# Attention and RWKV-style mixing with layer norms on one core: inputs laid out by channel, VectorE's 32x32 transposes in place of TensorE's, ScalarE normalising the result, new places in the order

## The chip, the cores and the metric

One core of a Trainium2 chip runs the whole program. Time is device time in microseconds; the kernel before takes 707.49 us, the median of three runs (705.98 to 707.81). TensorE is also called PE, VectorE DVE, ScalarE ACT, GpSimd POOL and the SyncE queue SP, as in the profile.

## The reference, cut to what matters

Sixteen sequences x of 512 tokens by 128 channels, 16 heads of 8 channels, all in f32:

```python
h = x @ W1 + b1                      # 128 -> 384, per head q, k, v of 8 channels
w = softmax(causal(q @ k.T / sqrt(8)))
x = layernorm(x + (w @ v) @ Wp + bp)
x_prev = x shifted by one token
xr, xk = mu_r*x + (1-mu_r)*x_prev, mu_k*x + (1-mu_k)*x_prev
out = sigmoid(xr @ W_r.T) * (relu(xk @ W_k.T)**2 @ W_v.T)
x = layernorm(x + out)
```

## The kernel before, in words

Each sequence is a batch element and passes through seven stages, each one step behind the last: X (x is loaded and transposed), A (q and k, split into three bf16 parts that go out to memory and come back as operands), S (row maxima of the scores, and v), T (scores again, transposed, exponentials, product with v), D (division by the sums, projection, first layer norm, transpose), E (key, gate, value), F (second layer norm and store). `OFFSET` tells which batch element a stage has in step b. A step has ten groups g, five for each half of the heads; a group has two places.

The order of each engine is written out by hand, and every engine takes its instructions strictly in that order. TensorE does in each group, twice: a pair of T chunks (`t_chunks`, L559) into one of three banks `tps`, the masks and score matmuls of a pair of S chunks (L582, L597) into one of three banks `sps`, then whatever `SPARE_USES` puts at this place; and behind the second the product with v of the group before (`pv`, L624). A pair of S chunks waits by `bank_free` until all but the last chunk ahead of it is reduced.

VectorE does in each group: `reduce_chunk` 0 and 1 (L843), the small work of place 0, layer norm pieces, `reduce_chunk` 2 and 3, the work of place 1. ScalarE takes the exponentials of each T pair (L765), then copies of spare results. GpSimd does its pieces of the group and at its end the causal mask of the group's exponentials (`mask_group`, L1023), which `pv` needs.

All small matmul results share one PSUM bank, `spare`: each use waits until the one ahead of it is read. Seven of the fourteen uses per step are transposes by TensorE against an identity: xT (four of 128x128), max0 and max1 (row maxima of a half, 128x32), sums0 and sums1 (the unnormalised attention output of a half with its sums, four each), attnT (four), hT (four); the other uses are the matmuls q, k, v, project, key, gate and value.

The maxima of a half: TensorE transposes them, ScalarE negates them into `negmax` (L747), GpSimd splits them into two bf16 parts (`split_max`, L1036 and L1038), SP writes them to memory and loads them back as rows of `qop` (`load_max`, L388). The attention output of a half: ScalarE copies it (`copy_o`), TensorE transposes it, VectorE takes reciprocals and multiplies straight from PSUM (L873, L876); after both halves TensorE transposes once more and ScalarE copies attnT (L736). In group 4 VectorE adds bias and x into y (L882) and takes the moments; in group 5 GpSimd makes the inverse deviation (`inverse_deviation`, L1043 and L1045) and VectorE scales y to h in groups 5 and 6 (L894). The same helper scales z to the result in groups 3 and 5.

A step in the middle of the run repeats every 39.0 us. The first attention step has S only; after the last S step come one with T only and a finish written out by halves.

Of the kernel before, what the change touches and what calls it, by code (L numbers as in the profile page):

```python
# [26 lines left out]
BF16 = mybir.dt.bfloat16  # L27
# [4 lines left out]
P = 128  # L32
# [3 lines left out]
BLK = 128  # L36
HROWS = 64
# [12 lines left out]
MAXIMA = QUARTET * NQBLK  # L50
LOADED = 16 * 2 * 2
# [9 lines left out]
FIRST_STEP, LAST_STEP = -3, 17  # L61
# [9 lines left out]
}  # L71
LATE = ("T", "D", "E", "F")
EARLY_OPS = (("k", 0), ("xT", 1))
# [31 lines left out]
MOVED = {("sums1", BATCH - 1): (1, 1), ("attnT", BATCH - 1): (2, 1), ("key", BATCH - 2): (2, 0)}  # L105
# [28 lines left out]
def shifted(b, g, by):  # L134

    at = GROUPS * b + g + by
    return at // GROUPS, at % GROUPS, 0
# [42 lines left out]
def block_program(nc, x, W1, b1, Wp, bp, Wr, Wk, Wv, mu_r, mu_k, consts, out):  # L180
    with ExitStack() as ctx:
# [14 lines left out]
        w1 = sb("w1", [E, 3 * E])  # L196
        w1p = sb("w1p", [E, 3, E])
        wff = sb("wff", [E, 3, E])
        wffT = sb("wffT", [E, 3, E])
        wp = sb("wp", [E, E])  # L200
# [3 lines left out]
        bias = sb("bias", [P, 2 * E])  # L204
        vcol = sb("vcol", [E, 1])
        mus = sb("mus", [P, 2])
        half_power = sb("half_power", [P, TT])

        xa = sb("xa", [P, TT, E])
# [9 lines left out]
        negmax = sb("negmax", [MAXIMA, P])  # L219
        negmax_parts = sb("negmax_parts", [MAXIMA, MROWS, P], BF16)  # L220
# [3 lines left out]
        inv = sb("inv", [P, 2, TT, QUARTET, 2])  # L224
        attn = sb("attn", [P, TT, HEADS, DH])
# [7 lines left out]
        rstd = sb("rstd", [P, 2, TT])  # L233
        h = sb("h", [P, 2, TT, E])
# [39 lines left out]
        xa_in = sem("xa_in")  # L274
# [10 lines left out]
        s_reduced = sem("s_reduced")  # L285
        max_high = sem("max_high")
# [7 lines left out]
        o_copied = sem("o_copied")  # L294
        inv_done = sem("inv_done")
        xbias_done = sem("xbias_done")
# [13 lines left out]
        rstd2_done = sem("rstd2_done")  # L310
        result_done = sem("result_done")
# [63 lines left out]
        def _(sp):  # L375
            sp.dma_start(xa[:], x[0].rearrange("(t p) e -> p t e", p=P)).then_inc(xa_in, 16)
# [87 lines left out]
        def _(pe):  # L464
            def setup_rest():

                pe.wait_ge(weights_in, 16 * 7)
                for i in range(3):
                    last = nc.tensor.transpose(tps[:, 0, E * i:E * i + E], wff[:, i, :], ident)
# [675 lines left out]
```

## Time and profile before

| | |
|---|---|
| median of three runs | 707.49 us |
| profiled execution | 709.11 us |
| its span, first to last instruction | 707.4 us |
| mean granted TensorE clock | 0.935 of full |
| PE, DVE, ACT, POOL busy | 611.5, 546.1, 450.6, 415.5 us |
| DMA moved | 65.80 MB |

Busy time is the time in which an engine has an instruction under way; matmuls overlap, so a busy PE is not PE at its peak. The clock is 1.0 at 2.4 GHz and 0.5 at 1.2 GHz. In the timeline rows, the number in brackets is idle time of the engine before the instruction, with what ended it.

### The profile page before, as it was taken

The numbers are of one execution on the slowest core, as the hardware profiler recorded it, in microseconds if no ns is written. First come the engines' busy times: TensorE is split into PE (matmuls) and PEld (weight loads), VectorE is DVE, ScalarE is ACT, GpSimd is POOL, SyncE is SP. The second block draws the span as 40 slices with busy tenths as digits, with TensorE's granted clock in tenths as the row PEclk, the third lists the DMA queues.
The fourth block names the chain that finished last, engine by engine and source line by source line (L and its number), as shares of the span: only waits on it lengthen the run. The fifth ranks groups of instructions, "written<-read, shape, count | busy, mean of one in ns | idle before, by whom it ended". The sixth has DMA issues, their size and how long they took to land.

```text
span 707.4 us, 17691 instructions
## 1 busy us (share of the span) xinstructions
PE 611.5 (86%) x6729; PEld 273.8 (39%) x6729; DVE 546.1 (77%) x1654; ACT 450.6 (64%) x871; POOL 415.5 (59%) x548
## 2 busy tenths in 40 slices
PE   4458889989998999999899989989999999897963
PEld 2123333334343434444343434444443434342432
DVE  1386778789897988888897979888888979793237
ACT  2103777676767676767767677767677676666731
POOL 3011325565748485766757484857667575758473
PEclk9555999999999999999999999999999999997987
DMA  4752544333443535353334535353433335201100
GB/s 136 126 136 46 143 71 141 68 113 67 107 119 63 136 78 151 77 145 79 114 77 103 127 60 140 78 150 79 138 80 118 78 77 133 53 4 32 31 16 30
DMA packets 72202, 65.80 MB, mean 93 GB/s; under 512 B 9333, under 2 KB 63926, under 8 KB 72118
## 3 DMA queue, kind: packets, MB, share of 16 engines
q1 hardware_dynamic: 71410, 64.41, 38.3%
q8 instruction: 53, 0.87, 0.6%
q10 hardware_dynamic: 708, 0.26, 0.3%
q14 instruction: 31, 0.25, 0.1%
HBM read 34.70 MB, written 29.88 MB: 91 GB/s over the span
## 4 chain that ended last, share of the span: by engine, by line
PE 67%; DVE 20%; POOL 4%; ACT 4%; issue 3%; DMA 1%; ACTq 1%; POOLq 0%; SPq 0%; DVEq 0%
PE ops L624 18%; PE sps L597 13%; DVE rowmax L843 10%; PE tps L559 10%; PE spare L482 9%; PE spare L502 5%; PE sps L582 5%; DVE attn L876 2%; PE spare L534 2%; ACT probs L765 2%; DVE stats L849 2%; DVE y L882 1%; PE spare L497 1%; PE spare L523 1%; POOL probs L1023 1%
## 5 line engine op out<-in xcount | busy, mean ns | idle before, releaser
L843 DVE TENSOR_REDUCE rowmax<-sps 128x1 f32<-128x512 f32 (+7 forms) x1024 | 400.9, 450 | 85.7 <-PE sps L597 84.1
L765 ACT ACTIVATE probs<-tps 128x512 f32<-128x512 f32 x640 | 347.7, 597 | 122.6 <-PE tps L559 122.4
L1023 POOL TENSOR_SCALAR_AFFINE_SELECT probs<-probs 128x512 f32<-128x512 f32 x256 | 158.1, 636 | 205.6 <-ACT probs L765 204.2
L624 PE MATMUL ops<-probs,vop 128*32 128x384 f32 (+3 forms) x2048 | 175.6, 450 | 6.3 <-POOL probs L1023 5.8
L559 PE MATMUL tps<-qop,kop 50*128 50x384 bf16 (+3 forms) x1024 | 127.3, 307 | 13.7 <-ACT probs L765 11.2
L597 PE MATMUL sps<-kop,qop 48*64 48x512 bf16 (+7 forms) x2048 | 130.4, 310 | 8.1 <-DMA kop<-d_parts 8.1
L582 PE MATMUL sps<-qmask,dup 64*128 64x128 bf16 (+1 forms) x640 | 70.0, 215 | 27.1 <-DVE rowmax L843 24.5
L624 PEld LDWEIGHTS ops<-probs,vop 128*32 128x32 f32 x2048 | 50.7, 110 | 91.6 <-issue 62.2
L559 PEld LDWEIGHTS tps<-qop,kop 50*128 50x128 bf16 x1024 | 34.3, 94 | 125.6 <-ACT probs L765 82.9
L1030 POOL TENSOR_TENSOR qk_parts<-qk_rest,qk_parts 128x512 bf16<-128x512 f32 x32 | 36.8, 1152 | 46.8 <-ACT qk_parts L775 46.8
L597 PEld LDWEIGHTS sps<-kop,qop 48*64 48x64 bf16 x2048 | 43.1, 106 | 47.5 <-issue 18.5
L582 PEld LDWEIGHTS sps<-qmask,dup 64*128 64x128 bf16 x640 | 31.4, 95 | 75.9 <-DVE rowmax L843 71.7
L1055 POOL TENSOR_SCALAR scaled<-step_d,mus 128x512 f32<-128x512 f32 x30 | 47.2, 1573 | 1.5
L502 PE MATMUL spare<-xT,w1p 128*128 128x512 f32 x62 | 39.6, 724 | 2.7 <-ACT xT L727 2.7
L865 DVE SCALAR_TENSOR_TENSOR qk_rest<-spare,bias,qk_parts 128x512 f32<-128x512 f32 x31 | 23.3, 751 | 21.4 <-ACT qk_parts L743 21.4
L1057 POOL TENSOR_TENSOR mixed<-scaled,hT 128x512 f32<-128x512 f32 x30 | 38.0, 1266 | 2.5
L743 ACT ACTIVATE qk_parts<-spare,bias 128x512 bf16<-128x512 f32 x31 | 21.3, 688 | 27.5 <-PE spare L502 27.5
L1045 POOL TENSOR_TENSOR rstd<-vareps,half_power 128x4 f32<-128x4 f32 x30 | 31.5, 1050 | 2.5
L534 PE MATMUL spare<-mixed,wffT 128*128 128x512 f32 x28 | 16.7, 680 | 13.6 <-DVE attn L876 13.6
L873 DVE RECIPROCAL inv<-spare 128x32 f32<-128x32 f32 x32 | 11.2, 349 | 21.5 <-PE spare L518 21.5
L518 PE MATMUL spare<-cst,osum 128*128 128x128 f32 x128 | 21.9, 296 | 1.6 <-ACT osum L771 0.8
L482 PE MATMUL spare<-w1p,xT 128*128 128x128 f32 x128 | 19.4, 297 | 3.6 <-DVE attn L876 3.6
(123 smaller groups left out, 571.7 us busy)
## 6 DMA issues: line engine op xcount, KB each, us to landing
qop<-d_parts SPq DMA_DIRECT2D x64, 192.0 KB, 4.5
kop<-d_parts SPq DMA_DIRECT2D x63, 192.0 KB, 5.3
d_parts<-qk_parts SPq DMA_DIRECT2D x15, 768.0 KB, 3.4
d_parts<-qk_parts SPq DMA_DIRECT2D x15, 512.0 KB, 4.4
d_parts<-qk_parts SPq DMA_DIRECT2D x17, 256.0 KB, 4.6
xa<-L_attn_x SPq DMA_DIRECT2D x16, 256.0 KB, 2.8
xres<-L_attn_x SPq DMA_DIRECT2D x16, 256.0 KB, 3.1
out<-result SPq DMA_DIRECT2D x15, 256.0 KB, 2.4
```

Source lines behind the costliest of these rows:

```text
L482: last = nc.tensor.matmul(spare[:, P * t:P * t + P], tokensT[:, P * t:P * t + P], weights, start=True, stop=True)
L502: last = nc.tensor.matmul(spare[:], w1p[:, "qk".index(use), :], xT[:, n % BANKS], start=True, stop=True)
L559: last = nc.tensor.matmul(tps[:, bank(n + k), off:off + w], kop[r, par, pair, BLK * a:BLK * a + BLK], qop[r, par, pair, BLK * a:SEQ], star ...
L582: nc.tensor.matmul(dst, dup[r, :], src, start=True, stop=False, skip_group_check=True)
L597: last = nc.tensor.matmul(sps[out:out + QBLK, bank(n + k), off:off + w], qop[r, par, pair, QBLK * a:QBLK * a + QBLK], kop[r, par, pair, 0: ...
L624: last = nc.tensor.matmul(ops[32 * t:32 * t + 32, BLK * a:SEQ], vop[:, par, a, QUARTET * half + t, hh, :], probs[:, g % 2, i, off:off + w] ...
L765: nc.scalar.activation(probs[:, g % 2, i, :], tps[:, bank(n), :], ACT.Exp, scale=SCALE)\
L843: last = nc.vector.reduce_max(rowmax[:, par, QUARTET * half + i, a:a + 1], sps[:, bank(n), off:off + w], axis=AX_X)
L1023: last = nc.gpsimd.affine_select(out=v, in_=v, compare_op=ALU.is_ge, fill=0.0, base=0, pattern=[[0, QUARTET], [1, BLK]], channel_multiplie ...
L1030: nc.gpsimd.tensor_tensor(part(i, 2), qk_rest[:, i, :], part(i, 1), ALU.subtract).then_inc(qk_split, 1)
L1055: nc.gpsimd.tensor_scalar(scaled[:], step_d[:], mus[:, i:i + 1], None, ALU.mult).then_inc(scaled_done, 1)
L1057: nc.gpsimd.tensor_tensor(mixed[:, i, :], scaled[:], hT[:, 0:SEQ], ALU.add).then_inc(mixed_done, 1)
```

## The change

- Host: x comes a second time transposed per sequence, and is loaded straight into xT; W1 comes sorted into q, k, v; the feed-forward weights come transposed; biases and mu come as one table of columns. The stage X has no TensorE or ScalarE work left, and the first step, -3, is gone.
- Maxima: VectorE turns the 128x32 maxima in 32x32 squares (`turn_maxima`), in group 5 and in group 0 of the next step, behind the group's first two reductions. They are no longer negated; the constant rows that meet them are -1. GpSimd splits them at the start of groups 5 and 0. Four DMAs take the place of one on the way out.
- Attention output: VectorE turns 128x512 in squares (`turn_sums`, groups 2 and 7), takes reciprocals, divides (`divide`, groups 3 and 8) and turns back straight into attnT (`turn_back`, group 3).
- The second layer norm's scaling goes to ScalarE (groups 4 and 5), as scale and shift; GpSimd makes the shift.
- Places: v, hT, gate, value, ksq, z, the mixing and the splits of q and k move by a group or a place.

```diff
-FIRST_STEP, LAST_STEP = -3, 17
+FIRST_STEP, LAST_STEP = -2, 17
 SPARE_USES = {
-    ("X", "xT"): (6, 1),
     ("A", "q"): (0, 1), ("A", "k"): (1, 1),
-    ("S", "v"): (9, 0), ("S", "max0"): (6, 0),
-    ("T", "max1"): (1, 0), ("T", "sums0"): (8, 1),
-    ("D", "sums1"): (2, 0), ("D", "attnT"): (3, 0), ("D", "project"): (4, 0), ("D", "hT"): (8, 0),
-    ("E", "key"): (2, 1), ("E", "gate"): (5, 0), ("E", "value"): (7, 0),
+    ("S", "v"): (8, 1),
+    ("D", "project"): (4, 0), ("D", "hT"): (7, 0),
+    ("E", "key"): (2, 1), ("E", "gate"): (3, 1), ("E", "value"): (5, 1),
 }
...
@@ sync @@
-            sp.dma_start(xa[:], x[0].rearrange("(t p) e -> p t e", p=P)).then_inc(xa_in, 16)
+            sp.dma_start(xT[:, 0], xT_in[0]).then_inc(xT_loaded[0], 16)
...
-                sp.dma_start(d_max[half].rearrange("i h r q -> r i h q"),
-                             negmax_parts[:].rearrange("r i (h q) -> r i h q", h=2)).then_inc(max_out, 16)
+                for hh in range(2):
+                    for part in range(2):
+                        r = HROWS * hh + SQUARE * part
+                        sp.dma_start(d_max[half, :, hh, :, SQUARE * part:SQUARE * part + SQUARE].rearrange("i r q -> r i q"),
+                                     max_parts[r:r + SQUARE]).then_inc(max_out, 16)
...
@@ scalar @@
+            def normalise(n, half):
+                wait(act, shift2_done, n + 1)
+                wait(act, stored, 16 * n)
+                for t in tiles_of(half):
+                    last = nc.scalar.activation(result[:, t, :], z[:, t, :], ACT.Identity, bias=shift[:, t:t + 1],
+                                                scale=rstd[:, 1, t:t + 1])
...
@@ vector @@
+            def turn_maxima(n, half):
+                wait(dve, s_reduced, 4 * GROUPS * n + 2 * GROUPS * (half + 1))
+                wait(dve, max_split, 2 * n + half)
+                nc.vector.transpose(maxT[:], rowmax[:, n % 2, QUARTET * half:QUARTET * half + QUARTET, :].rearrange(
+                    "p a b -> p (a b)")).then_inc(max_turned, 1)
+            def turn_sums(n, half):
+                m = 2 * n + half
+                wait(dve, o_copied, m + 1)
+                wait(dve, attn_done, m)
+                nc.vector.transpose(turned[:].rearrange("q b s h d -> q (b s h d)"), osum[:, half, :])\
+                    .then_inc(turned_done, 1)
+                wait(dve, turned_done, m + 1)
+                nc.vector.reciprocal(inv[:, half], turned[:, :, 1, :, 0]).then_inc(inv_done, 1)
+            def divide(n, half):
+                m = 2 * n + half
+                wait(dve, inv_done, m + 1)
+                wait(dve, attnT_done, n)
+                nc.vector.tensor_tensor(attn[:, :, half], turned[:, :, 0],
+                                        inv[:, half].unsqueeze(3).to_broadcast([P, SQUARES, 2, DH]), ALU.mult)\
+                    .then_inc(attn_done, 1)
+            def turn_back(n):
+                wait(dve, attn_done, 2 * n + 2)
+                is_written(dve, "project", n - 1)
+                nc.vector.transpose(attnT[:], attn[:].rearrange("q b s h d -> q (b s h d)")).then_inc(attnT_done, 1)
...
@@ vector, step(b), behind reduce_chunk 0 and 1 @@
+                    if g == CHUNKS and active("S", b):
+                        turn_maxima(before("S", b), 0)
+                    if g == 0 and active("S", b - 1):
+                        turn_maxima(before("S", b - 1), 1)
                     for _, use, n in ORDER[b, g, 0]:
                         spare_use(use, n)
+                    if tg == 2 and active("D", tb):
+                        turn_sums(before("D", tb), 1)
+                    if tg == 3 and active("D", tb):
+                        divide(before("D", tb), 1)
+                        turn_back(before("D", tb))
+                    if tg == CHUNKS + 2 and active("T", tb):
+                        turn_sums(before("T", tb), 0)
+                    if tg == CHUNKS + 3 and active("T", tb):
+                        divide(before("T", tb), 0)
...
-                    if tg in (3, 5) and active("F", tb) and before("F", tb) < LAST - 1:
-                        n = before("F", tb)
-                        wait(dve, stored, 16 * n)
-                        normalise(1, n, (tg - 3) // 2, z, result, rstd2_done, result_done)
...
@@ gpsimd, step(b) @@
+                    if g == CHUNKS and active("S", b):
+                        split_max(before("S", b), 0)
+                    if g == 0 and active("S", b - 1):
+                        split_max(before("S", b - 1), 1)
                     if tg == 0 and active("E", tb) and before("E", tb) < LAST:
-                        mix_sum(before("E", tb), 0)
+                        mix_add(before("E", tb), 0)
                     if tg == 1 and active("F", tb) and before("F", tb) < LAST - 1:
                         inverse_deviation(1, before("F", tb), moments2_done, vareps2_done, rstd2_done)
+                        shift_of(before("F", tb))
-                    if g in (2, 3) and active("A", b):
-                        split_low(before("A", b), g - 2)
+                    if g in (3, 4) and active("A", b):
+                        split_low(before("A", b), g - 3)
...
-                    if tg == 4 and active("E", tb) and before("E", tb) < LAST:
+                    if tg == 3 and active("E", tb) and before("E", tb) < LAST:
                         n = before("E", tb)
                         is_read(pool, "key", n)
...
                     if tg == 5 and active("D", tb) and before("D", tb) < LAST:
                         inverse_deviation(0, before("D", tb), moments_done, vareps_done, rstd_done)
-                    if tg == 8 and active("E", tb) and before("E", tb) < LAST - 1:
+                    if tg == 6 and active("E", tb) and before("E", tb) < LAST - 1:
...
+                    if tg == 8 and active("D", tb) and before("D", tb) < LAST:
+                        mix_step(before("D", tb))
+                        mix_scale(before("D", tb), 1)
                     if tg == 9 and active("D", tb) and before("D", tb) < LAST:
-                        mix_step(before("D", tb))
-                        mix_sum(before("D", tb), 1)
+                        mix_add(before("D", tb), 1)
+                        mix_scale(before("D", tb), 0)
```

## Rows read from the trace of the kernel before

**Rows 1.** The page, part 1: busy us and share of the span.
```profile
PE 611.5 (86%) x6729; PEld 273.8 (39%) x6729; DVE 546.1 (77%) x1654; ACT 450.6 (64%) x871; POOL 415.5 (59%) x548
```

**Rows 2.** The page, part 4: the chain that ended last, by engine.
```profile
PE 67%; DVE 20%; POOL 4%; ACT 4%; issue 3%; DMA 1%; ACTq 1%; POOLq 0%; SPq 0%; DVEq 0%
```

**Rows 3.** Windows of one steady step: length, busy us of PE, PEld, DVE, ACT, POOL, clock, DMA.
```profile
294.00:333.00 39.00, 36.28 (x424) 16.49 (x420) 33.47 (x102) 27.89 (x55) 26.12 (x35) 1.00 0.43 105
```

**Rows 4.** Timeline of PE, groups 2 and 5 to 7 of a steady step: start, us, instruction.
```profile
302.37 0.66 PE L518 MATMUL spare<-cst,osum 128*128 128x128 f32 x4
302.96 0.39 PE L559 MATMUL tps<-qop,kop 50*128 50x512 bf16 x2
...
304.86 1.12 PE L534 MATMUL spare<-mixed,wffT 128*128 128x512 f32 x2 [1.00 <-DVE attn L876]
...
313.45 0.39 PE L559 MATMUL tps<-qop,kop 50*128 50x512 bf16 x2
314.41 0.20 PE L582 MATMUL sps<-qmask,dup 64*128 64x64 bf16 x2 [0.57 <-DVE rowmax L843]
...
318.50 0.28 PE L478 MATMUL spare<-cst,rowmax 128*32 128x128 f32 x1
...
321.51 0.39 PE L559 MATMUL tps<-qop,kop 50*128 50x512 bf16 x2
```

**Rows 5.** Timeline of DVE in the same step.
```profile
303.81 0.35 DVE L873 RECIPROCAL inv<-spare 128x32 f32<-128x32 f32 x1
...
304.73 1.41 DVE L843 TENSOR_REDUCE rowmax<-sps 128x1 f32<-128x384 f32 x4
...
312.03 0.69 DVE L882 TENSOR_TENSOR y<-spare,xbias 128x512 f32<-128x512 f32 x1 [0.37 <-PE spare L482]
...
314.99 1.29 DVE L843 TENSOR_REDUCE rowmax<-sps 128x1 f32<-128x512 f32 x2 [0.30 <-PE sps L597]
316.23 0.60 DVE L894 TENSOR_SCALAR h<-y,moments,rstd 128x128 f32<-128x128 f32 x2
```

**Rows 6.** Groups by form: busy us, mean ns, of a 128x256 tensor operation.
```profile
L967 DVE TENSOR_TENSOR step_d<-hT 128x256 f32<-128x256 f32 x2 | 0.8, 414 | 0.0
```

**Rows 7.** Timeline of POOL in the same step.
```profile
314.75 0.24 POOL L1043 TENSOR_SCALAR vareps<-moments 128x4 f32<-128x4 f32 x1
315.07 1.05 POOL L1045 TENSOR_TENSOR rstd<-vareps,half_power 128x4 f32<-128x4 f32 x1
...
322.19 0.29 POOL L1036 TENSOR_SCALAR negmax_parts<-negmax 32x128 bf16<-32x128 f32 x1
322.56 0.42 POOL L1038 TENSOR_TENSOR negmax_parts<-negmax,negmax_parts 32x128 bf16<-32x128 f32 x1
```

**Rows 8.** Windows of other stretches, columns as in rows 3.
```profile
117.00:120.00 3.00, 1.97 (x28) 0.75 (x24) 2.66 (x11) 2.15 (x5) 2.50 (x4) 1.00 0.35 124
...
121.00:127.00 6.00, 6.00 (x45) 1.91 (x41) 4.28 (x12) 3.29 (x7) 1.93 (x4) 0.50 0.77 127
...
642.00:645.00 3.00, 1.22 (x16) 0.48 (x16) 0.00 (x0) 2.26 (x5) 2.93 (x4) 1.00 0.00 0
...
646.00:656.00 10.00, 8.15 (x31) 2.19 (x34) 1.49 (x7) 5.43 (x11) 6.95 (x11) 0.50 0.02 4
```

**Rows 9.** Timeline of PE in step 1, around the clock's fall.
```profile
117.10 0.39 PE L559 MATMUL tps<-qop,kop 50*128 50x512 bf16 x2
...
127.16 0.39 PE L559 MATMUL tps<-qop,kop 50*128 50x512 bf16 x2
```

**Rows 10.** Timeline of all engines at the start.
```profile
4.31 1.09 PE L497 MATMUL spare<-cst,xa 128*128 128x128 f32 x4 [4.31 <-DMA cst<-shape_constants]
...
8.12 2.07 PE L502 MATMUL spare<-xT,w1p 128*128 128x512 f32 x2 [2.73 <-ACT xT L727]
```

**Rows 11.** Timelines of ACT and PE in the tail.
```profile
682.00 0.59 ACT L771 COPY osum<-ops 128x512 f32<-128x512 f32 x1 [5.24 <-PE ops L624]
...
687.05 0.71 PE L652 MATMUL spare<-wp,attnT 128*128 128x128 f32 x4 [0.68 <-ACT attnT L736]
```

More of the change, by code:

```diff
@@ L491, in spare_use @@
                     pe.wait_ge(s_reduced, 4 * GROUPS * BATCH)
-                if use == "xT":
-                    wait(pe, xa_in, 16 * (n + 1))
+                if use in ("q", "k"):
+                    wait(pe, xT_loaded[n % BANKS], 16 * (n // BANKS + 1))
+                    if n == 0:
+                        pe.wait_ge(w1_in, 16)
+                    last = nc.tensor.matmul(spare[:], w1p[:, "qk".index(use), :], xT[:, n % BANKS], start=True, stop=True)
+                elif use == "v":
+                    last = tokens_by_weights(spare, xT[:, n % BANKS], w1p[:, 2, :])
+                elif use == "project":
+                    wait(pe, attnT_done, n + 1)
+                    last = tokens_by_weights(spare, attnT, wp[:])
+                elif use == "hT":
@@ L654, in by_weights @@
                 return last
-            is_read(pe, "attnT", LAST)
+            wait(pe, attnT_done, LAST + 1)
             for half in range(2):
@@ L722, in spare_use @@
                 spare = spares[k]
-                if use in ("max0", "max1"):
-                    wait(act, max_split, 2 * n + int(use[-1]))
                 is_written(act, use, n)
-                if use == "xT":
-                    ins = nc.scalar.copy(xT[:, n % BANKS], spare[:])
-                elif use == "v":
+                if use == "v":
                     if n == 0:
@@ L734, in spare_use @@
                                          spare[:].rearrange("k (a h d) -> k a h d", h=2, d=DH))
-                elif use == "attnT":
-                    ins = nc.scalar.copy(attnT[:], spare[:])
                 elif use in ("q", "k"):
@@ L742, in spare_use @@
                     wait(act, parts_out, 48 * (n - 1))
[L743 removed]
+                    nc.scalar.activation(part(i, 0), spare[:], ACT.Identity, bias=scalars[:, i:i + 1])\
                         .then_inc(qk_high, 1)
                     return
[L746 to L747 removed]
                 elif use == "hT":
@@ L864, in spare_use @@
                     wait(dve, qk_split, 2 * (n - 1) + i + 1)
-                    last = nc.vector.scalar_tensor_tensor(qk_rest[:, i, :], spare[:], bias[:, i:i + 1], part(i, 0),
+                    last = nc.vector.scalar_tensor_tensor(qk_rest[:, i, :], spare[:], scalars[:, i:i + 1], part(i, 0),
                                                           ALU.add, ALU.subtract)
-                elif use in ("sums0", "sums1"):
-                    half = int(use[-1])
-                    is_written(dve, use, n)
-                    is_written(dve, "attnT", n - 1, k)
-                    tiles = spare[:].rearrange("q (t r s h d) -> q s t r h d", t=TT, r=QUARTET, s=2, h=2)
-                    nc.vector.reciprocal(inv[:, half], tiles[:, 1, :, :, :, 0]).then_inc(inv_done, 1)
-                    wait(dve, inv_done, 2 * n + half + 1)
-                    for t in range(TT):
-                        last = nc.vector.tensor_tensor(
-                            attn[:, t, DH * half:DH * half + DH].rearrange("q (r h) d -> q r h d", h=2),
-                            tiles[:, 0, t], inv[:, half, t].unsqueeze(3).to_broadcast([P, QUARTET, 2, DH]), ALU.mult)
                 elif use == "project":
```

203 lines of the change are left out of this document (90 added, 113 removed).

## The prediction

> **What bounds the kernel now.** I read the page's busy shares first, then the chain of waits, then one steady step by windows, and last the timeline of that step engine by engine. TensorE is the busiest (86% of the span), VectorE second with 77% [rows 1], and the chain runs 67% through PE and 20% through DVE [rows 2]. A steady step lasts 39.0 us: the window of that length holds 36.28 us of PE, 33.47 of DVE, 27.89 of ACT, 26.13 of POOL, at full clock [rows 3]. So PE idles 2.7 us a step, and its longest gap is 1.00 us ahead of the key matmul, where it waits for VectorE's attn product [rows 4].
>
> The shares alone mislead. Scores live in three banks and go in pairs of chunks, 20 pairs a step. PE may start the mask matmul of a pair once VectorE has reduced the *first* chunk of the pair before (the idle of 0.57 us at 314.41 is this wait [rows 4]), and VectorE starts about 0.6 us after that mask matmul (314.41 to 314.99 [rows 4, 5]). A pair takes VectorE 1.41 us, or 1.29 [rows 5]. The two engines thus stay within one chunk of each other, and a pause of either longer than that is passed to the other. I carried this rule through the 20 pairs, with each engine's order and the durations of the rows: it gives 38.9 us for the step of before, where the rows say 39.0, so I use it for the changed order.
>
> **The change, part by part** (per steady step, unless said)
> 1. *PE.* Gone are the x, two sums and the attn transposes, four sets of four at 0.59 us (302.37 to the next instruction at 302.96), and two of the maxima at 0.28 [rows 4]: 4 x 0.59 + 2 x 0.28 = 2.9 us. The 1.00 us wait of key goes too, since no spare bank is held by the attn product. If PE set the step alone: 39.0 - 3.9 = 35.1.
> 2. *VectorE.* Gone: two times reciprocal and products (303.81 to 304.73, 0.92 us each) and the result's four scalings (as h's, 0.60 per two, 0.51 without overlap; [rows 5]) : 1.84 + 1.02 = 2.9 us. Added: three 32x32 transposes of 128x512. The trace has none. Below: 0.35, as the short reciprocal; above: 1.38, two passes at the 0.69 of the 128x512 sum; I take 0.65, the latter less overlap [rows 5]. Two divisions of 128x256 at 0.41 [rows 6], two reciprocals at 0.35, two 128x32 transposes at 0.18 (between nothing and 0.35), and five waits for its own results at 0.04: 1.95 + 0.82 + 0.70 + 0.36 + 0.20 = 4.0. Net +1.1: VectorE now carries about 34.6 to 35.0 and PE 33.4. The bound moves to VectorE.
> 3. *Coupling.* VectorE's new work falls behind the first pair of groups 2, 3, 7 and 8, each time ahead of the next reduction, and PE has nothing queued that it may do instead, because the S pair is next on its queue. Carried through the 20 pairs, and before part 4 is put in, PE now waits 0.4 to 0.6 us at most pairs and the step is 38.9 us: the 2.9 us off PE return as short waits. Gain 0.1.
> 4. *A new wait in group 5, the one that decides.* Before, POOL in group 5 makes 1/deviation right behind its mask: 314.75 plus 0.32, then 1.05 us, done at 316.12 [rows 7]; VectorE wants it for h at 316.23 [rows 5]: hidden by a hair. After, VectorE turns the maxima in group 5 *behind* its first two reductions; POOL's split of these maxima stands in group 5 *ahead* of 1/deviation; and VectorE's h stands directly behind its own turning. So h waits for a chain that starts only when VectorE reaches it: split 0.37 + about 0.33 (the second instruction is on 32 columns now, 0.42 before), then 0.32 + 1.05, and 0.14 of handovers = 2.2 us of VectorE standing still [rows 7]. What is queued behind it: h, reductions 2 and 3 of the group, gated; who waits: PE's masks of group 6. By hand, from the step's start: mask of group 5 at 21.2, turned at 23.2, h from 25.5 to 26.0, first reduction done 26.6; PE, ready for group 6's mask at 25.3, starts it at 26.7 and waits 1.2 us again at its second pair. Next step begins at 40.9. Bounds of the wait: 1.7 (both split instructions as short as vareps, 0.24) to 2.4 (the old durations); the step 40.4 to 41.1. Both conditions hold in steps 1 to 14: 14 times, +1.9 us each.
> 5. *TensorE's clock.* With the stall, PE in the stretch from 24.5 to 28.4 of the step works about 40% of the time, by the same table. Rows of before: behind 642:645 with 1.22 us of work in 3 the granted clock is 0.50, that is 1.2 GHz, and it fell once in the middle of the run too, behind 117:120 with 1.97 in 3; it then stood at half for 6 us of full work [rows 8]. What one fall costs is a difference of rows: group 5 to 7, from 117.10 to 127.16, took 10.06 us [rows 9], the same stretch of a steady step 313.45 to 321.51, 8.06 [rows 4]: +2.0 us. I take one fall in each of the 14 steps (from none to one): 42.9 us a step. Ends: 0 and +3.5 (all of PE's 6.4 us at half, nothing hidden).
>    The Trainium skill says the same of such kernels (TensorE: Matmul & The Clock Gate, A second HAM failure mode: psum-queue depth-cycling): cycling through PSUM banks leaves TensorE idle between groups often enough that the clock swings. By that rule every step falls, and the sum is as here; a reader who trusts the steady step more than the rule, whose gap of 1.00 us left the clock full, gets rival A.
> 6. *Other moves.* ScalarE loses the copies of xT and attnT and two of the maxima, and gains four scalings of 128x128: within 1 us of its 27.9, hidden since it has 11 us of idle [rows 3]; without that cover 0.3. POOL gains two tiny instructions and has mixing spread over groups 8, 9 and 0; mask(9) then ends about 1 us before PE wants it. Bound 0 to +0.5. SP: the maxima go out in four DMAs for one per half, some 1 us more issue and at most 1 us of landing; they are split two groups earlier and wanted half a step later; 0. The x load no longer waits for a transpose; 0. key, gate, value, hT, v earlier: PE does the same work in other groups, 0 to -0.2. Parts of q and k leave one group later, 3.5 us, with over 10 us to spare: 0.
> 7. *Start.* x transposes, ScalarE's table load and its copy stand between 4.31 and q at 8.12 [rows 10]. q can then start when x and W1 are in, an estimated 1.1 us after 4.31, so 2.7 earlier; but the table load stays in the chain, now in front of q's first activation. -2.0 (-2.7 to 0). The prologue step without attention: the turned maxima add 0.2, the x transposes leave 0.1: 0. Step 0 has no h and so no wait; it loses 1.7 us of PE transposes and adds about as much to VectorE as it drops: -0.5 (-1.7 to +0.5).
> 8. *Tail.* From the last osum copy (682.00) to the projection (687.05) are 5.05 us [rows 11]; copy 0.59, turn 0.69, reciprocal 0.35, divide 0.42, turn back 0.69 and hops 0.25 make 3.0: -2.0. Step 15 loses transposes where POOL and ACT partly cover them: -1.5 (0 to -4).
>
> Sum, against the profiled execution's 709.1: 14 x (1.9 + 2.0) = 54.6; -0.5 - 2.0 - 3.5 = -6.0; together 757.7. The profiled execution lies 1.6 above the median of the runs, so the forecast for the median is 756.
>
> **Rivals**
> - *A: the wait is there, the clock holds.* For: steady steps keep the full clock with a 1.00 us gap [rows 3, 4]. Against: the new stretch has less work than either stretch ahead of a fall, in proportion, or as little [rows 8]. 709.1 + 26.6 - 6.0 - 1.6 = 728.
> - *B, faster: the pause is absorbed.* If the pairs couple less than my table has it (a reduction freed earlier, PE further ahead), the step is VectorE's sum plus the wait, 35.0 + 2.2 = 37.2, 1.8 under 39.0: 709.1 - 25 - 6.0 - 1.6 = 676. The point from which it decides: VectorE's other idle, 3.6 us a step in my table, must fall under 1.7. Against it: the table reproduces 39.0, and VectorE idles 5.5 us a step before [rows 3]. If only the wait of part 4 were missing, the step stays 38.9 and the run comes to about 700.
> - *C: transposes of f32 take two passes.* 3 x 0.65 more on VectorE; by hand 0.9 a step beyond the wait, as part fills idle: 756 + 13 = 769. For it: no row has this operation. Against: every 128x512 operation of VectorE in the trace takes one pass, 0.69.
>
> **How the numbers follow.** Forecast 0.55, A 0.22, B 0.15 (676 to 704), C 0.08. A measurement tells about 0.3% from no change; with that bound faster 0.16, same 0.03, slower 0.81. The range leaves out B and what of C and the full cost of the falls lies above: 712 to 772; the forecast's own is 742 to 770.
>
> **What would show it.** In the changed profile: DVE's h idle before it, released by POOL's rstd, about 2.2 us, 14 times; steps of 42 to 43 us; PEclk under 1.0 once a step; PE's share under 80% and DVE's share about 80%; 128x512 transposes near 0.7 us; no PE transposes but h's; key without its 1.00 us. I am wrong in the main step if h waits under 1 us or steps are under 39; wrong in the clock if PEclk stays at 1.0 from 80 to the tail; wrong in the rate if a transpose takes over 1 us.

## The result, and the profile after

The changed kernel takes 738.78 us (736.61 to 743.37, 4 runs) beside 707.65 (705.98 to 708.61) for the kernel before: ratio 1.0464, 95% interval 1.0427 to 1.050. Slower, inside the forecast's range and 17 us under its 756. The wait of part 4 is there at the size forecast. Part 5, the clock, is not the other half of the loss: it comes to some 6 us in place of 28, and a collision of VectorE with GpSimd, which the prediction did not have, stands beside it. Every ratio rests on executions that lie within 1.5% of the fastest of their kernel.

The page of the changed kernel: busy us, granted clock in 40 slices, the chain by engine [rows 1, 2].
```profile
PE 599.7 (81%) x6438; PEld 254.2 (34%) x6438; DVE 567.8 (77%) x1579; ACT 455.0 (61%) x862; POOL 415.6 (56%) x576
PEclk9999997697999999999999999999999999999975
PE 55%; DVE 27%; issue 7%; POOL 5%; ACT 4%; DMA 1%; DVEq 0%; POOLq 0%; SPq 0%; ACTq 0%
```
PE gave up 11.8 us of busy time, VectorE took on 21.7, and the chain moved from PE (67 to 55%) to VectorE (20 to 27%). VectorE's share stayed at 77%, because the span grew with the work.

What was waited for in the changed kernel: engine and line, releaser, us in total, times, longest.
```profile
PE sps L557 <- DVE rowmax L809: 68.2, 105, 2.5
DVE h L877 <- POOL rstd L1043: 33.0, 15, 2.5
```
The second row is part 4; the first is how it reaches PE. Timeline of VectorE in group 5 and 6 of a late step [rows 5].
```profile
416.53 0.20 DVE L848 STREAM_TRANSPOSE maxT<-rowmax 128x32 f32<-128x32 f32 x1
418.92 0.84 DVE L877 TENSOR_SCALAR h<-y,moments,rstd 128x128 f32<-128x128 f32 x2 [2.19 <-POOL rstd L1043]
```
The same on GpSimd [rows 7]: it waits for the turned maxima, splits them, and only then makes 1/deviation.
```profile
416.82 0.22 POOL L1028 TENSOR_SCALAR max_parts<-maxT 128x32 bf16<-128x32 f32 x1 [1.70 <-DVE maxT L848]
417.12 0.25 POOL L1030 TENSOR_TENSOR max_parts<-maxT,max_parts 128x32 bf16<-128x32 f32 x1
417.45 0.23 POOL L1041 TENSOR_SCALAR vareps<-moments 128x4 f32<-128x4 f32 x1
417.77 1.05 POOL L1043 TENSOR_TENSOR rstd<-vareps,half_power 128x4 f32<-128x4 f32 x1
418.79 0.64 POOL L1015 TENSOR_SCALAR_AFFINE_SELECT probs<-probs 128x512 f32<-128x512 f32 x1
```
TensorE pays in group 6 [rows 4]:
```profile
420.42 0.23 PE L557 MATMUL sps<-qmask,dup 64*128 64x128 bf16 x2 [1.39 <-DVE rowmax L809]
...
422.28 0.29 PE L557 MATMUL sps<-qmask,dup 64*128 64x128 bf16 x2 [0.96 <-DVE rowmax L809]
```

**Where the 34.2 us of span are** (741.6 against 707.4). The q matmul opens each step. The windows from q to q, after [rows 3]:
```profile
97.01:143.54 46.53, 39.22 (x388) 14.62 (x384) 32.97 (x90) 26.32 (x50) 21.08 (x29) 0.78 0.38 87
143.54:187.51 43.97, 38.10 (x406) 15.61 (x402) 35.17 (x99) 27.05 (x51) 24.42 (x32) 0.88 0.33 82
187.51:229.63 42.12, 35.60 (x406) 14.99 (x402) 35.10 (x99) 28.42 (x56) 26.11 (x36) 0.96 0.42 96
229.63:271.19 41.56, 34.32 (x407) 14.94 (x403) 35.11 (x99) 28.50 (x56) 26.12 (x36) 1.00 0.41 98
271.19:311.97 40.78, 35.74 (x406) 15.45 (x402) 34.33 (x99) 28.36 (x56) 26.16 (x36) 0.96 0.40 100
352.76:395.83 43.07, 35.87 (x407) 15.34 (x403) 35.09 (x99) 28.54 (x56) 26.10 (x36) 0.96 0.40 94
```
Twelve steps, from 97.01 to 602.15, take 505.1 us where before's twelve, from 100.77 to 568.38, took 467.6: +37.5. All ahead of them is 3.8 shorter, all behind them 0.4 longer. Now read clock against length. The step at full clock takes **41.56**, and one with a fall can take *less*, 40.78. What differs is VectorE's busy time: 35.11 against 34.33, 0.78 us, the very difference of the two lengths. It is one instruction pair, the h of group 6. VectorE in these two steps, the h of groups 5 and 6:
```profile
252.72 0.84 DVE L877 TENSOR_SCALAR h<-y,moments,rstd 128x128 f32<-128x128 f32 x2 [2.19 <-POOL rstd L1043]
...
256.61 1.36 DVE L877 TENSOR_SCALAR h<-y,moments,rstd 128x128 f32<-128x128 f32 x2
...
294.28 0.84 DVE L877 TENSOR_SCALAR h<-y,moments,rstd 128x128 f32<-128x128 f32 x2 [2.19 <-POOL rstd L1043]
...
298.16 0.59 DVE L877 TENSOR_SCALAR h<-y,moments,rstd 128x128 f32<-128x128 f32 x2
```
Counted from q, the first pair stands at 23.09 in both steps and the second at 26.98 and 26.97: the fall, from 21.3 to 24.7 us into the second step, has held VectorE up by nothing, and the lengths part at the second pair alone. GpSimd in the same stretches:
```profile
255.44 1.27 POOL L1092 TENSOR_TENSOR z<-gated,h 128x512 f32<-128x512 f32 x1 [2.21 <-DVE gated L842]
256.65 1.23 POOL L1015 TENSOR_SCALAR_AFFINE_SELECT probs<-probs 128x512 f32<-128x512 f32 x2
...
296.99 1.27 POOL L1092 TENSOR_TENSOR z<-gated,h 128x512 f32<-128x512 f32 x1 [2.21 <-DVE gated L842]
298.62 1.23 POOL L1015 TENSOR_SCALAR_AFFINE_SELECT probs<-probs 128x512 f32<-128x512 f32 x2 [0.37 <-ACT probs L726]
```
Each row of h and of masks is two instructions. In the long case the first h begins within 0.05 us of the first of two masks of GpSimd, and each h ends 0.08 us behind its mask, the second at 257.97 against 257.89. In the short case PE at half clock was late with the scores in group 6, so ScalarE's exponential came late, GpSimd stood idle for 0.37 us, and h got in between and took 0.59. At 418.92 one of two h waits likewise for the end of a mask (419.43): 0.84. The mean h was 354 ns before, 516 after. VectorE's reductions and its 128x512 transposes (0.70 us) took no longer beside a mask than without one.

The Trainium skill states a mechanism (SBUF — State Buffer, "SBUF: two separate sides"): VectorE in some modes and GpSimd take a shared port pair as an exclusive lock for a whole instruction, whichever of them starts first, and the other blocks fully. The rows agree with it in the end, 0.08 us behind the mask. They do not show the part on who starts first: in the long case the record of the first h begins 0.05 us ahead of the mask's, and h is the one held. No run here isolates the port.

### The profile page after: what moved, and what is told of

Read it like the earlier page. It is cut to its first block, busy times and chain, and to the rows that moved or that the text cites. A ratio compares the mean times of both kernels' runs of the same rounds, so it can differ in the third digit from the quotient of the medians.

```text
span 741.6 us, 17178 instructions
## 1 busy us (share of the span) xinstructions
PE 599.7 (81%) x6438; PEld 254.2 (34%) x6438; DVE 567.8 (77%) x1579; ACT 455.0 (61%) x862; POOL 415.6 (56%) x576
## 4 chain that ended last, share of the span: by engine, by line
PE 55%; DVE 27%; issue 7%; POOL 5%; ACT 4%; DMA 1%; DVEq 0%; POOLq 0%; SPq 0%; ACTq 0%
DVE rowmax L809 16%; PE ops L599 16%; PE sps L572 12%; PE spare L481 7%; PE tps L534 7%; PE sps L557 5%; PE spare L495 5%; ACT probs L726 2%; POOL rstd L1043 2%; PE spare L509 2%; DVE stats L815 2%; DVE h L877 2%; DVE y L836 1%; DVE turned L856 1%; DVE moments L819 1%
## 5 line engine op out<-in xcount | busy, mean ns | idle before, releaser
L599 PE MATMUL ops<-probs,vop 128*32 128x384 f32 (+3 forms) x2048 | 186.5, 474 | 5.3 <-POOL probs L1015 4.1
L534 PE MATMUL tps<-qop,kop 50*128 50x384 bf16 (+3 forms) x1024 | 131.0, 315 | 34.9 <-ACT probs L726 34.1
L877 DVE TENSOR_SCALAR h<-y,moments,rstd 128x128 f32<-128x128 f32 x60 | 28.6, 516 | 33.0 <-POOL rstd L1043 33.0
L1053 POOL TENSOR_SCALAR scaled<-step_d,scalars 128x512 f32<-128x512 f32 x30 | 47.1, 1571 | 3.1
L1028 POOL TENSOR_SCALAR max_parts<-maxT 128x32 bf16<-128x32 f32 x32 | 7.0, 219 | 67.1 <-DVE maxT L848 67.0
L495 PE MATMUL spare<-xT,w1p 128*128 128x512 f32 x62 | 39.6, 724 | 4.5 <-DMA w1p<-W 4.5
L831 DVE SCALAR_TENSOR_TENSOR qk_rest<-spare,scalars,qk_parts 128x512 f32<-128x512 f32 x31 | 23.3, 751 | 19.7 <-ACT qk_parts L706 19.7
L706 ACT ACTIVATE qk_parts<-spare,scalars 128x512 bf16<-128x512 f32 x31 | 21.3, 687 | 27.7 <-PE spare L495 27.7
L856 DVE STREAM_TRANSPOSE turned<-osum 128x512 f32<-128x512 f32 x32 | 22.4, 700 | 16.0 <-ACT osum L732 16.0
L1092 POOL TENSOR_TENSOR z<-gated,h 128x512 f32<-128x512 f32 x14 | 17.8, 1269 | 29.5 <-DVE gated L842 29.5
L698 ACT COPY vop<-spare 128x512 f32<-128x512 f32 x16 | 9.4, 587 | 39.4 <-PE spare L481 39.4
```

The lines of the kernel that those rows point to most:

```text
L495: last = nc.tensor.matmul(spare[:], w1p[:, "qk".index(use), :], xT[:, n % BANKS], start=True, stop=True)
L534: last = nc.tensor.matmul(tps[:, bank(n + k), off:off + w], kop[r, par, pair, BLK * a:BLK * a + BLK], qop[r, par, pair, BLK * a:SEQ], star ...
L599: last = nc.tensor.matmul(ops[32 * t:32 * t + 32, BLK * a:SEQ], vop[:, par, a, QUARTET * half + t, hh, :], probs[:, g % 2, i, off:off + w] ...
L877: last = nc.vector.tensor_scalar(dst[:, t, :], src[:, t, :], moments[:, i, t, 0:1], rstd[:, i, t:t + 1], ALU.subtract, ALU.mult)
L1053: nc.gpsimd.tensor_scalar(scaled[:], step_d[:], mus[:, i:i + 1], None, ALU.mult).then_inc(scaled_done, 1)
```

## The experiments

Each stands against the kernel before, timed beside it on the same chip: 706.28 us for 1, 2, 4 and 6; 706.3 for 3, 5, 7 and 8; 706.04 for 9 and 12; 705.06 for 10 and 11. Ratios of different groups are compared only roughly. Steps are from q to q; kernel 1 is that of experiment 1, and so on.

**1. 1/deviation first.** The changed kernel with GpSimd's `inverse_deviation` of group 5 moved ahead of the split.
```diff
-                    if g == CHUNKS and active("S", b):
-                        split_max(before("S", b), 0)
                     ...
                     if tg == 5 and active("D", tb) and before("D", tb) < LAST:
                         inverse_deviation(0, ...)
+                    if g == CHUNKS and active("S", b):
+                        split_max(before("S", b), 0)
```


> The changed kernel with one edit: in group 5 GpSimd makes the inverse deviation ahead of the split of the maxima instead of behind it. Theory (the wait of h behind the split, 2.2 us in each of 14 steps, and the clock's falls that it brings): h waits under 0.1 us, a step falls from 42.1 us on average (40.8 where the clock holds) to 38.8 by the hand-carried table, the clock stays at 1.0 in the middle of the run; total 695 to 704 us, that is below the kernel before. Rival (VectorE is overloaded by its own transposes and the new places, and the wait only stands where it would idle anyway): at most a few us are won, total 730 or more.

704.68 us, ratio 0.9978 (0.9952 to 1.0004). Two windows of it:
```profile
211.93:250.73 38.80, 34.15 (x406) 14.93 (x402) 34.15 (x99) 28.37 (x56) 26.21 (x36) 1.00 0.44 106
250.73:291.05 40.32, 35.67 (x407) 15.46 (x403) 34.15 (x99) 28.38 (x56) 26.21 (x36) 0.96 0.42 100
```
One swap of two calls gives back the whole loss: h is at 362 ns and waits only once (2.5 us), so the swap takes away the wait and the collision together and does not tell them apart. It also shows parts 1 to 3: without the wait the 2.1 us less of PE's work bring 0.2 (39.00 to 38.80; by hand 38.9). The clock did not stay up as expected, it fell in two steps of the middle, and the total is 0.7 us over the range. So the run prices a fall of the clock that nothing hides: 1.5 us.

**2. Before, with the wait alone.** GpSimd's 1/deviation waits for the second reduction of group 5, close to where the turning of the maxima releases it after the change.
```diff
+                        wait(pool, s_reduced, 4 * GROUPS * before("S", b) + 4 * CHUNKS + 2)
                         inverse_deviation(0, before("D", tb), moments_done, vareps_done, rstd_done)
```


> The kernel before with only the wait put in: in group 5 GpSimd's inverse deviation first waits until VectorE has reduced the group's second chunk, so that VectorE's h finds it about 1.5 us late. Nothing else is changed. Theory: the table gives 40.4 us for a step of 39.0, so +20 us from the wait alone, 728, and up to 745 with falls of the clock. Rival (the transposes and places cost, not the wait; TensorE's queue covers a pause of VectorE): 707 to 712.

759.58 us, ratio 1.0744 (1.0697 to 1.0791): over the 728 to 745 expected. The wait itself is 24.0 us in 15, so 1.6 each.
```profile
266.80:310.19 43.39, 39.12 (x425) 17.30 (x421) 33.90 (x103) 28.14 (x55) 26.17 (x35) 0.92 0.38 93
310.19:352.50 42.31, 37.72 (x425) 16.88 (x421) 33.77 (x103) 28.13 (x55) 26.18 (x35) 0.96 0.40 96
```
The wait alone, with nothing else of the change, makes the kernel slower than the change does. Table 40.4, measured 42.3 with the clock at half for 3.4 us of the step, and 43.4 with 6.8 us. The first h also meets a mask (0.25 us more). PE still has its transposes here (37.7 to 39.1 us of work a step), which makes it likely that the falls are not hidden, but no full step of this run kept the clock, so how much of the +3.3 is wait and how much clock is argued from the table.

**3. A longer chain.** Three more small GpSimd instructions ahead of the split in group 5.
```diff
+                if half == 0:
+                    for k in range(3):
+                        nc.gpsimd.tensor_scalar(again[:, k], maxT[:], 1.0, 0.0, ALU.mult, ALU.add)
```


> The changed kernel with three more GpSimd instructions of the split's size in group 5, ahead of the split: the chain in front of h is longer by 3 x 0.3 = 0.9 us. Theory (every us of that chain stands in the step): h waits 3.1 us in place of 2.2, the table gives 41.6 for 40.7, 13 us more in all, and some more from the clock: 750 to 760. Rival (the wait is partly idle time that VectorE has anyway): under 5 us more than the changed kernel's 739.

763.98 us, ratio 1.0833 (1.0789 to 1.0878). They took 0.57 us together, not 0.9, and VectorE's wait grew from 2.19 to 2.71. Steps went to 42.7 and 42.9, later 44.5, with the clock at 0.96, 0.92 and 0.88: of +1.1 to +3.0 us a step over 41.56, 0.5 is the wait; the rest came with the falls (no step here kept the clock). The wait follows the chain; the total lies 4 us over the range.

**4. PE's work put back.** Kernel 1 with sixteen 128x128 transposes a step that nobody reads.
```diff
+                if use in ("v", "project", "hT", "value"):
+                    for t in range(TT):
+                        nc.tensor.transpose(spare[:, P * t:P * t + P], ident, ident)
```


> As e1, and TensorE gets 16 more 128x128 transposes a step (4 ahead of each of v, project, hT and value, into the shared bank, overwritten at once), 2.36 us, about the work that the change took from it. Theory (TensorE and VectorE are coupled pair by pair, VectorE is the fuller): the table gives 40.6 against 38.8 for e1, so about +25 us, since these four places are ones where VectorE's next pair is waited for. Rival (VectorE alone is the bound and TensorE idles 6 us a step): within 5 us of e1.

721.21 us, ratio 1.0206 (1.015 to 1.0261). 16.5 us over kernel 1, for about 25 expected. Steps at full clock 39.98, so +1.2 (table +1.8); with a fall 41.58, so 1.6 for one.
```profile
178.45:218.43 39.98, 35.73 (x422) 16.48 (x418) 34.09 (x99) 28.51 (x56) 26.16 (x36) 1.00 0.42 101
```
The sixteen transposes fill 1.58 us of PE (35.73 against 34.15), 0.40 per four, where part 1 counted 0.59 from start to start.

**5. Turns made twice.** Kernel 1 with the 128x512 transpose of each half done twice.
```diff
+                nc.vector.transpose(turned_again[:], osum[:, half, :])
                 nc.vector.transpose(turned[:].rearrange("q b s h d -> q (b s h d)"), osum[:, half, :])\
```


> As e1 (704.7), and VectorE's turn of the 128x512 attention output is done twice for each half, 2 x 0.63 us of VectorE a step more. Theory (pairwise coupling, VectorE the fuller engine but with waits of its own): the table gives 39.6 for 38.8, about +12 us, two thirds of the work added (20 us). Rival 1 (VectorE's sum is the bound): all of it, +20. Rival 2 (VectorE has slack, TensorE is the bound): under 5.

728.54 us, ratio 1.0316 (1.0273 to 1.036). 1.4 us more of VectorE a step makes the step at full clock 39.47, +0.67 (table 39.6); then the clock falls in nearly every step (41.00), in some twice (42.45). The total was missed, +24 us for +12, because the falls came in number, and here nothing covers them: 1.5 us each.

**6. `pv` inside the group.** Kernel 1 with `pv` at the first place of groups 2, 3 and 8 and q at (0, 0): TensorE then has work between the two pairs where VectorE has extra.
```diff
+                        if i == 0 and g in (2, 3, 8) and active("T", tb):
+                            pv(before("T", tb), tg - 1)
```


> As e1, with the same work in two other places of TensorE's queue: in groups 2, 3 and 8 the product with v stands between the group's two score pairs instead of behind both, where it followed a spare matmul directly; q moves to place 0 of group 0. Theory (the step is set by how far the two engines can run apart, not by either's sum): the table gives 37.0 for a step against 38.8, so 25 us less than e1: about 673. Rival (VectorE's sum is the bound, or GpSimd's masks come too late for the earlier products): no gain over e1, or a loss.

683.85 us, ratio 0.9661 (0.9608 to 0.9714): steps 36.90 at full clock (table 37.0), 38.44 with a fall. The step is as the table has it; the total is 11 us over the expected 673, with a fall in four of twelve steps. Part 3's coupling is what ate the gain: 1.9 us a step return when the order fits.

**7. Group 6 filled.** The changed kernel with ten idle matmuls of 128x512 in PE's waits of group 6.
```diff
+                        if g == CHUNKS + 1 and active("S", b) and active("D", b):
+                            fill(before("T", b), g, i)
```


> The changed kernel, and TensorE does 10 idle matmuls of 128x512 in group 6 of steps 1 to 14 while it waits for VectorE (6 ahead of the first score pair, 4 ahead of the second, into a score bank that the next chunk overwrites). The order and the wait of h stay. Theory (of the 39 us between the changed kernel and e1's order 28 are the wait and 10 to 14 the clock that falls in it): h still waits 2.2 us, the clock stays at 1.0 in the middle, steps of 40.8 to 41.0, total 724 to 730. Rival (the clock's falls are hidden behind VectorE, their price is nothing): 738 or more.

744.26 us, ratio 1.0538 (1.0475 to 1.0601). A miss on both counts. The clock still fell in every second step, half of the times from 21.3 us on, in group 5, behind two waits of 0.57 and 0.46 us and ahead of the filled ones. Steps with a fall took 42.0 and 42.15, and even those at full clock took 41.55, not 40.8.

**8. VectorE's small work spread.** Kernel 1 with the pieces placed singly between the 40 reductions of a step (only the two pairs of h stay together), places of the spare uses and `pv` shifted to match.
```diff
+VECTOR_AT = {'tm1': 1, 'qrest': 2, 'krest': 5, 'ts1': 7, 'rc1': 8, 'div1': 11, 'back': 14, 'y': 17, 'mom1': 19, 'gated': 21, 'tm0': 22, 'h0': 27, 'h1': 27, 'ts0': 32, 'rc0': 34, 'div0': 36, 'mom2': 39}
...
+                for slot in range(4 * GROUPS):
+                    reduce_chunk(before("S", b), slot // 4, slot % 4)
+                    for name, at in VECTOR_AT.items():
+                        if at == slot and work[name][0]:
+                            work[name][1]()
```


> As e1, with the same instructions in other places, chosen by the table: VectorE's small pieces stand singly between single reductions instead of together behind the second or fourth; q, k, key and value move to place 0 and hT to place 1 of their groups; the product with v stands inside groups 3, 7 and 8. Theory (the loss lies in how the two engines wait for each other pair by pair, not in their sums): 34.9 a step for 38.8, 14 x 3.9 = 55 less than e1: 650, at most 660, and the clock holds as TensorE is 93% busy. Rival (e6's gain of 21 was all that there is, ScalarE or GpSimd bound next): 675 to 685.

653.08 us, ratio 0.9249 (0.9204 to 0.9294), the best here.
```profile
203.03:238.61 35.58, 33.06 (x403) 14.72 (x403) 34.39 (x98) 27.96 (x55) 26.34 (x37) 1.00 0.45 114
```
VectorE works 34.39 of 35.58 us: now it is the bound, and the step is 3.4 us under before's 39.0. The edit moves TensorE's pieces too, and no run parts the two. Of VectorE's time 1.1 us a step is not work: one of the two divisions begins beside GpSimd's mixing and takes 1.49 us, where 0.41 is its time alone in the changed kernel.
```profile
232.03 1.49 DVE L877 TENSOR_TENSOR attn<-turned,inv 128x256 f32<-128x256 f32 x1
...
231.96 1.27 POOL L1073 TENSOR_TENSOR mixed<-scaled,hT 128x512 f32<-128x512 f32 x1
```
So the best order here still holds a collision of the kind that lengthened h.

**9. Groups 4 to 6 filled**, against experiment 7's open question.
```diff
-                        if g == CHUNKS + 1 and active("S", b) and active("D", b):
+                        if g in (CHUNKS - 1, CHUNKS, CHUNKS + 1) and active("S", b) and active("D", b):
```


> The changed kernel with idle matmuls of 128x512 (results overwritten, never read) ahead of TensorE's score masks: two at both places of group 4, three at both of group 5, six and four in group 6. This closes the two waits of about 0.5 us in group 5, behind which the clock fell even with group 6 filled, as well as those of 1.39 and 0.96 us in group 6. VectorE's order and its 2.2 us wait are untouched. If the falls cost what the same trace says (steps of 40.8 us where the clock stays up, 41.8 on average), the clock now stays at 1.0, every step is 40.8 to 41.0 and the run is 722 to 732. If the clock has no part in the length (steps above 40.8 have another cause), the run stays at 737 to 746 with the clock at 1.0. If filling brings no clock either, 740 to 750.

746.92 us, ratio 1.0575 (1.0537 to 1.0613).
```profile
223.45:265.76 42.31, 38.35 (x427) 16.66 (x423) 35.11 (x99) 28.60 (x56) 26.06 (x36) 1.00 0.39 96
```
The clock stays up in ten of twelve steps, and they take 42.31 each: no gain. The filler of group 4 stands where no wait was, so this run alone left its own cost open.

**10. Group 5 alone filled; 11. groups 5 and 6.** Two fillers at each place of group 5; in the second also five and three in group 6. The edit of kernel 11, against kernel 9:
```diff
-                for _ in range({4: 2, 5: 3, 6: 6 - i}[g]):
+                for _ in range(2 if g == CHUNKS else 5 - i):
```


> The changed kernel with two idle matmuls of 128x512 (overwritten, never read) ahead of TensorE's score masks at both places of group 5 only, where it waits 0.57 and 0.46 us for VectorE. They fit into these waits, so they cost nothing by themselves; the waits of 1.39 and 0.96 us in group 6 stay open. In the changed kernel the steps took 40.8 us where the clock stayed up and 42.1 on average over steps 3 to 14. If the clock falls because of the waits in group 5, and its fall is what lengthens these steps, the steps are 40.8, the clock is 1.0 and the run is 720 to 728. If the falls come from group 6 as well, 730 to 745 with the clock under 1.0.

> As the kernel with group 5 filled, and five and three idle matmuls ahead of the masks in group 6 too, so that nearly no wait is open in the stretch. Steps of 40.8 to 41.2 and 720 to 732 if the clock's falls are the rest of the slowdown and the filler hides in the waits; 738 or more at a clock of 1.0 if it was not the clock that made the steps longer than 40.8 but something else, or if even hidden filler costs. In the run with group 4 filled too, steps were 42.3 at a clock of 1.0, which leaves both open.

Kernel 10 spread widely: 740.29, 743.96, 752.05 and 763.48 us; its ratio, from the first two, is 1.0517 (1.0439 to 1.0594). Kernel 11 takes 740.11 us, ratio 1.0496 (1.0434 to 1.0558). Kernel 11:
```profile
180.09:221.65 41.56, 36.89 (x419) 15.93 (x415) 35.12 (x99) 28.50 (x56) 26.12 (x36) 1.00 0.39 97
304.78:346.92 42.14, 38.18 (x418) 16.05 (x415) 35.12 (x99) 28.50 (x56) 26.12 (x36) 0.96 0.41 97
```
Six of eleven steps keep the full clock and all six take 41.56 or 41.57, to the hundredth what the changed kernel's own full-clock step takes; 738 or more at a clock near 1.0 is the branch "not the clock". The profile of kernel 10 is of its run of 752.05 us, at a clock of 0.906 on average, but its five full-clock steps are 41.56 too. In neither does the clock fall at 21.3 us any more, where five of the changed kernel's falls were; behind the first step, those that are left come from 26.3 us on. In both VectorE is busy 35.12 us a step: h collides every time, as nothing delays GpSimd's mask. The expected 40.8 rested on reading the changed kernel's 40.8 steps as undisturbed ones; they are the ones in which a fall hides in VectorE's stall *and* breaks the collision.

**12. Spread, with the change's order on GpSimd.** Kernel 8 with the split ahead of 1/deviation again (the edit of experiment 1 reversed); VectorE now has five reductions between turning and h.

> The spread order (its run before: 653.08 us) with GpSimd's order of the change put back: the split of the maxima stands ahead of 1/deviation in group 5 again. VectorE now turns the maxima in slot 22 of 40 and scales h in slot 27, five reductions (over 3 us) later, and the chain split plus 1/deviation takes 2.2 us. If what costs is the distance on VectorE between what releases the chain and what waits for it, h waits under 0.5 us and the run is within 0.4% of 653. If the order on GpSimd itself costs (it delays mask and key's square behind the split), the run is 660 to 685.

667.01 us, ratio 0.9419 (0.9358 to 0.948), 14 over kernel 8. h no longer waits (0.8 us in all), yet the distance theory fails and the rival's range holds it: the step is 36.27, and 37.17 with a fall, which comes in five of twelve. GpSimd, in order, now stands at the split itself, and all behind it is late:
```profile
222.59 0.22 POOL L1044 TENSOR_SCALAR max_parts<-maxT 128x32 bf16<-128x32 f32 x1 [1.92 <-DVE maxT L857]
...
226.41 1.22 POOL L1031 TENSOR_SCALAR_AFFINE_SELECT probs<-probs 128x512 f32<-128x512 f32 x2
```
so that on VectorE the four h again meet the late z and mask, and take 1.85 us (1.42 in kernel 8):
```profile
226.11 1.85 DVE L889 TENSOR_SCALAR h<-y,moments,rstd 128x128 f32<-128x128 f32 x4
```

## Why the prediction was right, and where not

The direction and the main cause were right: by the forecast's own sum the wait alone gives 728, which is inside the range. That the time came within 17 us of 756 is partly luck, since 28 us for the clock were too much and the collision was missing.

- *Part 1, PE.* PE fell from 36.28 us a step to 34.32 at full clock: 2.0, not 2.9, since four transposes fill 0.40 and not 0.59 (experiment 4). The error cost nothing, as part 3 gave the gain away. Key's 1.00 us wait is gone.
- *Part 2, VectorE.* Taken 0.65, 0.18 and 0.41 for the transposes and the division; measured, by form:
```profile
L742 ACT ACTIVATE result<-z,shift,rstd 128x128 f32<-128x128 f32 x56 | 24.3, 490 | 0.0
L856 DVE STREAM_TRANSPOSE turned<-osum 128x512 f32<-128x512 f32 x32 | 22.4, 700 | 16.0 <-ACT osum L732 16.0
L865 DVE TENSOR_TENSOR attn<-turned,inv 128x256 f32<-128x256 f32 x32 | 15.5, 483 | 0.1
L848 DVE STREAM_TRANSPOSE maxT<-rowmax 128x32 f32<-128x32 f32 x32 | 6.5, 202 | 0.0
```
  One pass, so rival C falls. The division's 483 ns are a mean, mostly of 414 alone and 564 beside GpSimd's square of key. VectorE grew by 0.7 us a step without the collision (34.15 in kernel 1) and 1.6 with it; forecast 1.1.
- *Part 3, coupling.* Right: 38.80 without the wait (forecast 38.9). Experiments 6 and 8 show it from the other side.
- *Part 4, the wait.* Right: 2.19 us, 14 steps, and 40.78 (forecast 40.9) in the steps whose fall and missing collision leave the wait alone; the first pair of h, 0.84 us for 0.59, is in it. The lower bound was added wrongly: both split instructions at 0.24 give 2.0, not 1.7. Rival B falls.
- *Part 5, the clock: the step that failed.* Forecast one fall a step at +2.0, 28 us. Falls came in eight of the ten steps from 187.51 to 602.15, each 3.4 us long, but mostly not from the stretch that part 5 blamed. Five began 21.2 to 21.6 us behind q, in group 5, before PE's waits of 1.39 and 0.96 us in group 6; two began at about 26.4, as the second of these waits ended; one at 35.3. Two steps had the same waits and kept the clock. The price was a row of before whose fall lasted 6.8 us (120.3 to 127.1). An uncovered fall of 3.4 us costs 1.5 to 1.6 (experiments 1, 4, 5), also from 21.4 us on. In the changed kernel it depends on the place: from 21.2 to 21.4 us, in VectorE's stall of 2.2 us, it costs nothing and takes the collision away (40.78; at 21.6 us half of it, 41.12); from 26.4 it costs 0.5 (42.12, 42.09); from 35.3, 1.5 (43.07). The ten steps take 414.6 us, one *less* than ten at 41.56. The long falls of the first two steps (46.53 and 43.97; 20.5 and 10.2 us at half clock) cost 7.4 against two at 41.56; the same two steps of kernel 11, with one short fall each, take 41.20 and 42.10. So the clock made about 6 us net.
- *What stood in its place:* the collision, +0.78 in a step, which no part had. Per full-clock step: 38.80, +1.98 for the wait, +0.78 for h = 41.56. The split of the last two is read off the traces, no run takes the collision alone away; that every full-clock step of kernels 7, 10 and 11 is 41.56 too, at 35.1 us of VectorE, goes with it. Rival A (728: wait there, clock holding) is nearer to the mechanism than the forecast, and 11 us short. That 14 x 0.78 is 11 too is partly chance: the full collision stands in seven of the 14 steps, and falls of the clock lengthen others.
- *Part 6.* ScalarE's scalings took 490 ns each, 24.3 us in all, and were hidden as forecast (ACT 28.36 to 28.50 a step, from 27.89); no run tests them alone.
- *Part 7, start.* q starts at 4.52 instead of 8.12 [rows 10], the next q at 23.93 instead of 26.90: -3.0 (forecast -2.0). The 1.1 us that the forecast let pass from 4.31 to q were 0.2.
- *Part 8, tail.* Copy to projection:
```profile
716.72 0.59 ACT L732 COPY osum<-ops 128x512 f32<-128x512 f32 x1 [6.10 <-PE ops L599]
...
720.09 1.22 PE L627 MATMUL spare<-wp,attnT 128*128 128x128 f32 x4 [1.49 <-DVE attnT L872]
```
  3.37 us for 5.05 [rows 11]: -1.7 (forecast -2.0).

What stays open: which resource holds h and the division (the rows show the time only), how much of the loss the collision alone makes, and why the clock stays down so long in the first two steps.

## What to carry to other kernels

Before you put a piece of work on an in-order queue, ask what it waits for and what then stands behind it: here a split of 0.5 us, placed ahead of 1/deviation, cost the whole change, and swapping two calls gave it back. Relief on the busiest engine is worth nothing while a second engine is tied to it pair by pair; spread the new work of the second one singly between the pairs, and shift the first one's to match (0.925 of before), instead of in lumps. Price a clock fall by who is waiting for TensorE at that moment, and look at the full-clock steps first: if these are long, the clock is not the cause. Compare the mean time of the same instruction form before and after (h: 354 to 516 ns): where a form grew without a change of its own, look at what runs beside it.

## What the runs showed of the hardware that was not expected

- A VectorE scaling of 128x128 f32, SBUF to SBUF, that started with a GpSimd mask of 0.64 us ended 0.08 us behind it: two took 1.36 us in place of 0.59. A division of 128x256 with both inputs in SBUF took 1.49 us beside a GpSimd operation on two 128x512 tensors of 1.27 us (kernel 8), and 0.41 alone. Reductions from PSUM and 32x32 transposes were not lengthened.
- With group 6 filled the clock still fell behind two waits of 0.57 and 0.46 us in group 5; with both groups filled it stayed at 1.0 in six of eleven steps, with group 4 as well in ten of twelve. A fall of 3.4 us cost 0, 0.5 or 1.5 us by its place in the step.
- VectorE turned 128x512 f32 in 32x32 squares in 700 ns and 128x32 in 202; ScalarE's Identity with scale and shift on 128x128 f32, SBUF to SBUF, took 490 ns.
